# Folded or whole: how the squared quantisation errors of 16 units are summed

## The reference, cut to what matters

```python
for s in SHRINKS:                                  # 16 values, 0.4 to 1.0
    scale = base * s
    deq = clip(round(wb / scale), -15, 15) * scale
    err = sum((deq - wb) ** 2, axis=-1)            # over a block of 64 weights
    upd = err < best_err
    best_err, best_scale = where(upd, err, best_err), where(upd, scale, best_scale)
...
h = maximum(x @ w_fc_q.T, 0)
x = x + (h * h) @ w_proj_q.T
```

## Time and profile before

| what | us |
|---|---|
| timed runs | 451.8, 453.34, 455.67 |
| median of the three | 453.34 |
| profiled execution, its time | 452.77 |
| its span (first to last instruction) | 451.0 |
| end of the search: first matmul of `ffn2` | 174.03 |

### The profile page before, as it was taken

One profiled execution on the slowest core, in us unless ns is written; L12 is line 12 of the kernel. 1 busy time (PEld: TensorE's weight loads), 2 busy tenths in 40 slices (PEclk: granted clock), 3 DMA queues, 4 the chain that ended last, 5 costly groups with the idle time before them and its releaser, 6 DMA issues.

```text
span 451.0 us, 8463 instructions
## 1 busy us (share of the span) xinstructions
PE 372.2 (83%) x3278; PEld 277.3 (61%) x3278; DVE 334.8 (74%) x870; ACT 248.1 (55%) x371; POOL 164.0 (36%) x203
## 2 busy tenths in 40 slices
PE   2987897689979997997469959979899789996467
PEld 1554664345434456996357848858688677885356
DVE  4998599957995975367866976597868799569830
ACT  4889959778868982017545454665565754020000
POOL 3355844478979996000010132060502324011000
PEclk9998999869999999998759969999899998999598
DMA  9910000000000002400000000000000000000000
GB/s 265 362 61 2 0 0 1 0 1 1 0 1 1 0 0 55 134 1 1 0 2 1 1 1 1 1 14 1 13 0 15 1 15 1 13 1 3 12 15 12
DMA packets 11144, 11.42 MB, mean 25 GB/s; under 512 B 608, under 2 KB 10592, under 8 KB 11104
## 3 DMA queue, kind: packets, MB, share of 16 engines
q1 hardware_dynamic: 11104, 10.88, 7.6%
HBM read 9.83 MB, written 1.05 MB: 24 GB/s over the span
## 4 chain that ended last, share of the span: by engine, by line
PE 40%; DVE 25%; ACT 12%; POOL 11%; issue 10%; DMA 1%; POOLq 0%; DVEq 0%; ACTq 0%
PE pair L729 11%; PE pair L693 8%; POOL arena L336 7%; PE pair L555 5%; PE pair L664 4%; PE pair L715 3%; POOL arena L319 3%; DVE arena L1232 2%; PE pair L677 1%; DVE i L1431 1%; PE pair L515 1%; PE pair L393 1%; ACT arena L1063 1%; DVE arena L1227 1%; DVE arena L1506 1%
## 5 line engine op out<-in xcount | busy, mean ns | idle before, releaser
L336 POOL TENSOR_TENSOR arena<-arena 128x512 f32<-128x512 f32 x64 | 91.1, 1434 | 53.0 <-ACT arena L940 21.4
L729 PE MATMUL pair<-EU,arena 128*128 128x256 f32 x256 | 62.0, 400 | 11.4 <-DVE arena L1512 9.3
L693 PE MATMUL pair<-arena,EDT 128*128 128x256 f32 x256 | 60.3, 385 | 4.0 <-ACT arena L1071 4.0
L729 PEld LDWEIGHTS pair<-EU,arena 128*128 128x128 f32 x256 | 50.9, 202 | 18.8 <-DVE arena L1506 11.5
L377 POOL TENSOR_TENSOR arena<-arena 128x512 f32<-128x512 f32 x20 | 26.1, 1327 | 90.6 <-ACT arena L1063 90.6
L1232 DVE TENSOR_REDUCE arena<-arena 128x16 f32<-128x512 f32 x64 | 42.7, 678 | 20.7 <-POOL arena L336 20.6
L515 PE MATMUL pair<-QP,nidentr 128*128 128x512 f32 x144 | 46.9, 450 | 13.1 <-ACT arena L937 10.4
L693 PEld LDWEIGHTS pair<-arena,EDT 128*128 128x128 f32 x256 | 47.2, 190 | 11.6 <-ACT arena L1071 5.4
L515 PEld LDWEIGHTS pair<-QP,nidentr 128*128 128x128 f32 x144 | 27.1, 203 | 25.6 <-issue 18.0
L940 ACT ACTIVATE arena<-pair 128x1024 f32<-128x1024 f32 x32 | 33.4, 1043 | 13.9 <-PE pair L522 13.9
L522 PE MATMUL pair<-arena 128*128 128x512 fp8e4 x128 | 40.3, 398 | 0.0
(11 more groups left out here) (195 smaller groups left out, 649.7 us busy)
## 6 DMA issues: line engine op xcount, KB each, us to landing
arena<-in_L_ffn_e_down_dram SPq DMA_DIRECT2D x1, 2048.0 KB, 12.2
EU<-in_L_ffn_e_up_dram SPq DMA_DIRECT2D x1, 2048.0 KB, 8.1
arena<-in_L_ffn_w_fc_dram SPq DMA_DIRECT2D x2, 512.0 KB, 5.3
X<-in_x_dram SPq DMA_DIRECT2D x1, 1024.0 KB, 6.0
arena<-in_L_ffn_w_proj_dram SPq DMA_DIRECT2D x1, 1024.0 KB, 13.7
GUW<-in_fside_BxS2xS_dram SPq DMA_DIRECT2D x1, 1024.0 KB, 11.5
out_dram<-arena SPq DMA_DIRECT2D x8, 128.0 KB, 2.2
CTX<-in_ctx_dram SPq DMA_DIRECT2D x1, 512.0 KB, 4.9
```

Source lines behind the costliest of these rows:

```text
L336: pool.tensor_tensor(qf(g), sq[:, :, 0:32], sq[:, :, 32:64], ALU.add).then_inc(s["folded"], 1)
L693: last = pe.matmul(bk2(4 + i % 2)[:, r, :], EDT[:, k, at:at + P], xT4[:, b % 2, k, :], start=(k == 0), stop=(k == 1))
L729: last = pe.matmul(bk2(7)[:, n, :], PR[:, n, e, :], EU[:, e, :], start=(e == 0), stop=(e == EROWS - 1))
```

## The change

Units g with `g - 2 in FFN1_UNIT` (31, 33, ... 61, after which POOL squares a piece of the first layer) are called *whole*. For them POOL's fold falls away, and DVE waits for `squared` and sums all 64 columns of each block straight from `qd`. ACT, before it writes `qd` again, waits for `reduced` of a whole unit instead of `folded`. `folds(g)` counts the units up to g that are still folded. POOL still waits for `squared` of a whole unit before it squares the piece.

```diff
+        def whole(g):
+            return g - 2 in FFN1_UNIT
+        def folds(g):
+            return sum(not whole(i) for i in range(g + 1))
...
                 pool.wait_ge(s["squared"], g + 1)
-                if g >= DEEP:
-                    pool.wait_ge(s["reduced"], g - DEEP + 1)
...
-                pool.tensor_tensor(qf(g), sq[:, :, 0:32], sq[:, :, 32:64], ALU.add).then_inc(s["folded"], 1)
+                if not whole(g):
+                    if g >= DEEP:
+                        pool.wait_ge(s["reduced"], g - DEEP + 1)
...
+                    pool.tensor_tensor(qf(g), sq[:, :, 0:32], sq[:, :, 32:64], ALU.add).then_inc(s["folded"], 1)
...
                 if g >= 3:
-                    act.wait_ge(s["folded"], g - 2)
+                    if whole(g - 3):
+                        act.wait_ge(s["reduced"], g - 2)
+                    else:
+                        act.wait_ge(s["folded"], folds(g - 3))
...
             def sum_error(g):
-                dve.wait_ge(s["folded"], g + 1)
-                dve.tensor_reduce(err[:, g // NS % 2, :, g % NS], qf(g), AX.X, ALU.add
-                                  ).then_inc(s["reduced"], 1)
+                if whole(g):
+                    dve.wait_ge(s["squared"], g + 1)
+                    squares = blocks(qd[g % 3])
+                else:
+                    dve.wait_ge(s["folded"], folds(g))
+                    squares = qf(g)
+                dve.tensor_reduce(err[:, g // NS % 2, :, g % NS], squares, AX.X, ALU.add).then_inc(s["reduced"], 1)
```

More of the change, by code:

```diff
@@ L330, in _ @@
                 pool.wait_ge(s["squared"], g + 1)
-                if g >= DEEP:
-                    pool.wait_ge(s["reduced"], g - DEEP + 1)
-                if g == QF_LATE:
-                    pool.wait_ge(s["edT_t"], EROWS // 2)
-                sq = qd[g % 3].rearrange("p (b n) -> p b n", b=NBLK)
-                pool.tensor_tensor(qf(g), sq[:, :, 0:32], sq[:, :, 32:64], ALU.add).then_inc(s["folded"], 1)
+                if not whole(g):
+                    if g >= DEEP:
+                        pool.wait_ge(s["reduced"], g - DEEP + 1)
+                    if g == QF_LATE:
+                        pool.wait_ge(s["edT_t"], EROWS // 2)
+                    sq = qd[g % 3].rearrange("p (b n) -> p b n", b=NBLK)
+                    pool.tensor_tensor(qf(g), sq[:, :, 0:32], sq[:, :, 32:64], ALU.add).then_inc(s["folded"], 1)
                 if g % NS == 12 and g // NS + 1 < NCH:
```

## The result

| | kernel before | changed kernel |
|---|---|---|
| median of 20 runs each, us | 453.67 | 451.73 |
| lowest to highest | 451.8 to 456.0 | 449.77 to 453.72 |
| ratio, with its 95% interval | | 0.9955, 0.9938 to 0.9973 |
| profiled execution, its span | 451.0 | 449.3 |
| start of `ffn2` | 174.03 | 172.11 |

I forecast 454.7 us, 1.9 more than the profiled execution of before; measured are 1.9 less (0.45%, interval 0.27% to 0.62%). That lies in my range, but the sign is wrong.

The account below looks back on a forecast made before the run. From unit 31 on, a full PE was taken to alternate with a DVE backlog around each choice of scales, then POOL's last piece before `ffn2`. +1.5 + 1.6 - 1.2 = +1.9 us on 452.77 gave 454.7 us, range 451.0 to 458.7.

Parts of the forecast that it names:

- The sum's price: DVE's sums in 16 units: 1024 columns instead of 512 cost +0.52 us each, 8.4 us in all.
- The first backlog: Units 31 to 41, DVE behind after unit 32: ACT's squares wait for DVE's long sums, +1.5 us.
- DVE's blocked time: What DVE's instructions take above their duration with POOL idle: 8.0 us in the first backlog, 2.8 expected to go.
- The second backlog: Units 48 to 56: the square of unit 54 waits for the sum of 51 and comes 2.0 us late, +1.6 us.
- The end: Start of `ffn2`: without the folds of 59 and 61 POOL's last squared piece comes early, -1.2 us.
- Beyond: After `ffn2`'s start: everything later follows PE, so the sum is carried over as it is.
- The clock: Rival: PE's new waits, at some of units 36 to 45 and 54 to 57, lower its clock; +3.1, 457.8 us, chance 0.10.
- No relief: Slower rival: DVE's blocked time stays 8.0 and 3.5 us in the two backlogs; +5.9, 458.7 us, chance 0.20.
- Full relief: Faster rival: DVE hardly blocked, ACT's 4.06 us wait for the scaled chunk vanishes; -5.3, 447.5 us, chance 0.08.

Follow-up runs that it names:

- e6: Changed kernel, but POOL still folds the whole units too, into slots nobody reads, and ACT waits for both; 456.23 us, ratio 1.0074.
- e7: Changed kernel, but whole units sum only the first 32 columns of each block; 451.91 us, ratio 0.9977.
- e3_tail: Changed kernel with only units 57, 59 and 61 whole, the others folded as before; 450.26 us, ratio 0.9939.
- e2_after: The changed kernel as it is, measured again against the kernel before; 452.44 us, ratio 0.9991.
- e5_no_backlog: Changed kernel with only units 43, 45, 47, 57, 59 and 61 whole, outside both backlogs; 450.46 us, ratio 0.9928.
- e4_ring4: Changed kernel with a fourth tile for the squares from unit 31 on, so ACT waits for unit g - 4; 446.57 us, ratio 0.9888.
- e9_ring4_again: Changed kernel with the fourth tile for the squares, same text measured a second time; 449.40 us, ratio 0.9896.
- e8_fill: Kernel before with six products nobody reads in PE's wait before `ffn2`, leaving 0.22 us of wait; 450.74 us, ratio 0.9963.
- e11_half_fill: Kernel before with five shorter products nobody reads before `ffn2`, leaving 1.27 us of wait; 450.75 us, ratio 0.9963.
- e10_fill_after: Changed kernel with five products nobody reads in PE's wait before `ffn2`, leaving 0.18 us; 452.27 us, ratio 0.9978.
- c2: Kernel before, unchanged, one of four more profiled executions to see how often the clock falls at `ffn2`; no time given.
- c3: Kernel before, unchanged, another of the four further profiled executions for the clock at `ffn2`; no time given.
- c4: Kernel before, unchanged, the last of the four further profiled executions for the clock at `ffn2`; no time given.
- e1_before: The kernel before as it is, measured and profiled again as a control; 452.53 us, ratio 1.0003.

## Why the prediction was right or wrong

**The sum's price: right.** 1.21 us against 0.69 at the old width is the +0.52 taken.

**The first backlog: wrong by 1.5.** The stretch of units 32 to 48 costs nothing, 38.73 against 38.72. Four long sums did come in and `choose` did start earlier (by 0.72 us; I had 0.8). What failed is the sentence "If DVE's blocked time falls like the share, 8.0 x (1 - 60/92) = 2.8 us go": it fell from 7.7 to 3.1, by 4.6. The sum of unit 39, the first in the row at 123.69, ended at 124.9, which is 127.4 with the head start of 2.53 added; I had 128.9. So the lateness that I foresaw ended before `absolute`, inside the 4.06 us that ACT had waited in the earlier trace rows. The blocked time did not go by POOL's share but, it seems, by which instructions meet: at 92% it was 7.7 us, at 84% (`e6`, 20.09 of 24) 4.5, at 55% (the changed kernel) 3.1, and in `e7`, with less work on DVE and POOL busy 12.13 of 24 us, 5.6. I know of no way to read it from the share.

**The second backlog: right.** The square of 54 came 2.2 us late against its place behind unit 48 (2.0 forecast), and units 48 to 63 cost +1.56 (1.6 forecast). Its terms held as well: `choose` begins 1.69 us earlier (up to 1.56 forecast), and blocked time up to the sum of 51 fell by 1.1 (1.2 forecast). PE is 1.7 to 1.8 us late by unit 59; at unit 63, whose square no longer waits for POOL's fold of 60, 1.56 of that are left.

**The end: right.** PE's wait is 1.30 us for ACT's square instead of 2.42; the forecast was about 1.1, and the stretch behind the square of 63 got 1.0 us shorter where I had 1.2. `e3_tail` has the gain with only three whole units: 29.44 and 1.26 against 29.55 and 2.22. The sum in the search was then to be +1.9 and is +0.6: 1.5 of the difference lies in the first backlog, and the end gives 0.2 back.

**Beyond: wrong, and with it the sign.** "Everything later follows PE; I carry the sum over as it is" is the step that failed. It puts whatever comes after the start of `ffn2` at nothing. In four of six profiled executions of the kernel before the clock was low after PE's 2.42 us of idle time in front of `ffn2`, and in neither of the changed one after its 1.30. The profile that I worked from is one of the two in which it did not fall. So a cost was missing from the time of before, not from the change: 1.4 to 1.6 us in perhaps two executions of three, some 1.0 us in the mean (an estimate from the six profiles; the filler products measured 1.7). Added to what each version does in the search, it can be held against what the runs measured:

| us against before | search | with 1.0 for the clock | measured, interval |
|---|---|---|---|
| the change, first measurement | +0.6 | -0.4 | -2.0, -2.8 to -1.2 |
| the change again (e2_after) | +0.6 | -0.4 | -0.4, -1.5 to +0.7 |
| e3_tail | -1.1 | -2.1 | -2.8, -4.0 to -1.5 |
| e5_no_backlog | -1.6 | -2.6 | -3.3, -4.8 to -1.8 |
| e6_still_fold | +4.3 | +3.3 | +3.4, +2.1 to +4.6 |
| e7_half | +0.7 | -0.3 | -1.0, -2.4 to +0.3 |
| e4_ring4 | -4.0 | -5.0 | -5.1, -7.0 to -3.2 |
| e9_ring4_again | -4.0 | -5.0 | -4.7, -6.9 to -2.5 |
| e8_fill and e11_half_fill | 0.0 | -1.0 | -1.7, -2.9 to -0.5 |
| e10_fill_after | +0.6 | -0.4 | -1.0, -2.3 to +0.4 |

All but the first row lie in their intervals, which are 2 to 4 us wide; without the clock's term the fillers, `e3`, `e5` and `e7` would not. The fillers show that what PE does in this wait is worth time. They do not show that 1.0 us is all of it: if the clock fell in every execution of before, or with the 1.7 of the fillers, the change would be at -1.0 to -1.1, near the edge of the first interval. What else is in that one is open; the low clock that no profile located, and scatter of the kernel before, are the candidates on record.

The clock was among my rivals, with the wrong sign: I looked for new falls at the new waits, and argued against it from "the 2.92 us of idle before 126.23 did not lower the clock". That row is one execution. In four of the five repeats the clock fell after the same wait too, without a cost, since ACT sets the pace there; they are the four in which it fell at `ffn2`.

The Trainium skill, "TensorE: Matmul & The Clock Gate", section "Why this matters for your kernels", warns of gaps between bursts of matmuls. The traces agree with the warning, but not with the size: a gap of 2.42 us, shorter than those that the page warns of, was enough in four of six executions. One of 1.30 us or less was enough in none of eleven.

**"No relief"** was the rival that `e6` put to the test: +4.3 in the search and 1.0074 in time (3.4 us), where I had priced it at +5.9. Late squares themselves seem to keep POOL from its work (busy 20.09 of 24 us), so the loss would limit itself; no run tests that. **"Full relief"** is not what happened either: DVE was freed of more than half, but ACT's new wait for the sums took the place of its 4.06 us. With the fourth tile, -4.0 of my -5.3 come out.

**What stays open.** What decides between an execution with the fall and one without: the two without it are also the two whose low clock ahead of unit 31 lasted 10.2 us and not 3.4, so it need not be chance. Then the fall's share of all executions, of which six profiles tell little; where the changed kernel's other low clock goes; and why two measurements of one pair differ by 0.36%.

## What to carry to other kernels

Moving work from an engine that is seldom waited for to one with a backlog can hang on the depth of the buffer in between: here three tiles gave +0.6 us in the search and four gave -4.0. DVE's blocked time did not scale with POOL's share here, so measure it for the new order of instructions instead of scaling it. Before a dense burst on PE, a wait of a few us can cost more than its length: look at the granted clock behind it in several executions, and if the wait must stay, fill it with products that nobody reads.

## What the runs showed of the hardware

PE's granted clock differs between executions of the same program at the same wait: 2.42 us of idle before `ffn2` were followed by 1.00 in two executions and by 0.72 to 0.79 over the window of 6 us in c2, c3 and c4. The square of unit 32 also begins up to 2.5 us earlier or later in one and the same kernel, more than this change does. The falls ahead of it differ: the low clock of the earlier trace rows lasted 10.2 us in the first profile of before and 3.4 in the changed kernel's. Its length alone does not set the start, as `e1_before` had 3.4 us too and began at 102.53.

DVE's blocked time falls on whatever instruction stands there: the rounding in `quantise` took 1778 ns in the changed kernel and 695 in `e6`, while scaling took 1217 and 2062. The sums never showed it: 0.65 to 0.69 us for 512 columns and 1.20 to 1.22 for 1024 everywhere, with or without POOL at work. The Trainium skill, "SBUF — State Buffer", section "Who interferes with whom", has it that `tensor_reduce` never takes the shared pair of ports; these rows agree.
